# A two-layer pair kernel: x in halves from two queues, pair bias issued by ACT, third u ahead of the scores, channels innermost in the first centering, and idle TensorE products

## The reference

```python
x = x + attention(_gn(x), ...)         # 4 heads of 32
x = x + triangle(_gn(x), ...)

def attention(x):                      # layer norm, then
    xn = (x - mu) * rsqrt(var + 1e-05) * ln_gamma + ln_beta
    tri_bias = einsum('bijc,hc->bhij', xn, w_bias)
    q, k, v = projections of xn        # q scaled by 1/sqrt(32)
    scores = einsum('biqhd,bikhd->bihqk', q, k) + tri_bias[:, None] + mask_bias
    o = einsum('bihqk,bikhd->biqhd', softmax(scores), v) * sigmoid(xn wg + bg)
    return o wo + bo

def triangle(z):                       # layer norm, then
    a, b = mask * sigmoid(gate) * projection, twice
    x = einsum('bikh,bjkh->bijh', a, b)
    return sigmoid(zn g + g_b) * (layernorm(x) z_w + z_b)
```

## Time and profile before

| | us |
|---|---|
| median of 3 runs | 285.29 (284.13 to 285.58) |
| the profiled execution | 284.4 |
| its span | 282.6 |
| busy PE / DVE / ACT / POOL | 226.4 / 210.6 / 209.2 / 144.4 |

### The profile page before, as it was taken

The page is one execution under the profiler, slowest core; times in us unless marked ns, Lnnn a source line. Parts: engine busy times, 40 slices in busy tenths (PEclk is TensorE's granted clock), DMA queues, the critical chain, the costliest instruction groups (busy, mean ns, idle before and its releaser), DMA issues.

```text
span 282.6 us, 6859 instructions
## 1 busy us (share of the span) xinstructions
PE 226.4 (80%) x2394; PEld 182.6 (65%) x2394; DVE 210.6 (75%) x368; ACT 209.2 (74%) x953; POOL 144.4 (51%) x132
## 2 busy tenths in 40 slices
PE   0589492469999999999999999999669599677930
PEld 0579230347888878888788887888459566376930
DVE  4047962357999999999999999998545739959790
ACT  0566643279999999999999999999545645569590
POOL 5400000008876777767777677766200019998081
PEclk9999668579999999999999999999958689965695
DMA  8400033534454643554445553330000000000038
GB/s 130 63 11 2 1 112 121 171 124 142 145 171 170 221 163 132 199 181 165 165 149 195 184 186 118 117 115 2 0 2 0 0 2 2 1 1 2 0 49 118
DMA packets 42389, 27.09 MB, mean 96 GB/s; under 512 B 24404, under 2 KB 42356, under 8 KB 42356
## 3 DMA queue, kind: packets, MB, share of 16 engines
q1 hardware_dynamic: 36572, 25.95, 28.8%
q10 hardware_dynamic: 5784, 0.71, 1.7%
HBM read 1.36 MB, written 1.18 MB: 9 GB/s over the span
## 4 chain that ended last, share of the span: by engine, by line
PE 31%; issue 27%; ACT 21%; DVE 12%; POOL 4%; SPq 3%; POOLq 1%; DMA 0%; DVEq 0%; ACTq 0%
ACT maps L659 17%; PE psum L1181 7%; PE psum L1060 3%; PE psum L1192 3%; PE psum L1145 2%; SPq L392 2%; DVE u_full L951 2%; PE psum L1248 2%; PE psum L1171 2%; DVE shared L991 2%; PE psum L1226 2%; PE psum L1231 2%; PE psum L1146 1%; PE psum L1148 1%; PE psum L1257 1%
## 5 line engine op out<-in xcount | busy, mean ns | idle before, releaser
L659 ACT ACTIVATE maps<-psum,neg_max 96x96 f32<-96x96 f32 x384 | 123.9, 353 | 4.9 <-DVE neg_max L928 4.1
L490 POOL TENSOR_TENSOR maps<-maps,rden 96x768 f32<-96x768 f32 x48 | 70.5, 1469 | 81.5 <-DVE rden L938 75.3
L659 ACT ACTIVATION_READ_ACCUMULATOR maps<-psum,neg_max 96x1 f32 x384 | 83.9, 219 | 0.0
L944 DVE COPY turned<-psum 96x1024 f32<-96x1024 f32 x48 | 58.5, 1219 | 8.4 <-PE psum L1181 8.4
L928 DVE TENSOR_REDUCE neg_max<-psum 96x8 f32<-96x768 f32 x48 | 45.7, 953 | 5.1 <-PE psum L1148 4.9
L1145 PE MATMUL psum<-u_st,x_stack 128*96 128x384 f32 x96 | 37.8, 394 | 10.4 <-DVE bias_lo L913 8.1
L1181 PE MATMUL psum<-ident,maps 96*96 96x96 f32 x384 | 40.0, 247 | 0.3 <-POOL maps L490 0.3
L1146 PE MATMUL psum<-bias_hi,ident_r 128*96 128x384 f32 x96 | 33.7, 351 | 0.0
L1148 PE MATMUL psum<-bias_lo,ident_r 128*96 128x384 f32 x96 | 33.4, 348 | 0.0
L1181 PEld LDWEIGHTS psum<-ident,maps 96*96 96x96 f32 x384 | 32.0, 126 | 0.5 <-POOL maps L490 0.5
L1145 PEld LDWEIGHTS psum<-u_st,x_stack 128*96 128x96 f32 x96 | 15.9, 166 | 19.8 <-issue 10.5
(11 more groups left out here) (178 smaller groups left out, 424.1 us busy)
## 6 DMA issues: line engine op xcount, KB each, us to landing
u_st<-u_split SPq DMA_DIRECT2D x96, 192.0 KB
x_stack<-shared SPq DMA_DIRECT2D x40, 96.0 KB, 2.0
maps<-in_x SPq DMA_DIRECT2D x4, 288.0 KB, 5.1
x_stack<-shared SPq DMA_DIRECT2D x4, 144.0 KB, 2.1
out_y<-maps SPq DMA_DIRECT2D x6, 96.0 KB, 3.1
out_y<-maps ACTq DMA_DIRECT2D x6, 96.0 KB, 3.4
bias_lo<-gate_sb SPq DMA_DIRECT2D x24, 12.0 KB
x_stack<-shared SPq DMA_DIRECT2D x4, 48.0 KB, 1.9
```

The lines of the kernel that those rows point to most:

```text
L490: pool.tensor_tensor(at, at, rden[:, rows, :].unsqueeze(3).to_broadcast([N, 2, H, N]), ALU.mult).then_inc(probs_ready, 1)
L659: e = act.activation(probs[:, k % SLOTS, n, h], bank_s[r % 4][0:N, h * N:(h + 1) * N], ACT.Exp, bias=neg_max[:, r % BODY, h:h + 1], accum_ ...
L944: dve.tensor_copy(turned[0:N, j % 2].rearrange("p r x -> p (r x)"), psum[0:N, 2 * BANK:4 * BANK]).then_inc(t_ready, 1)
```

## The change

- x is loaded in two halves (12 of 24 blocks each): SP issues members 0 and 1, ACT members 2 and 3, ahead of its other loads. TensorE waits for each half by itself.
- The pair bias's four transfers are issued by ACT, behind its last bias copy, and no longer by SP behind `stage(0)`.
- The third u (`u_projection(2)`, its high and low part) comes ahead of the first scores, no longer behind the second.
- Layer 0's centred values lie as (f c) in the banks, as layer 1's do; the reduction reads them contiguously, the normalization writes them to the old place in (c f).
- TensorE gets products of `ones_r` and `tri_b`, 96 by 192, whose results nobody reads: 40 before x, 8 before the first means, 10 before the first centering, 20 before the first transposes, 36 before the first scores; in layer 1, 6 and 6 around the last output, 8 and 9 ahead of variance and centering, 28 behind the centering and 3 between quads of transposes. For them `ones_made` tells TensorE that `ones_r` is set.

```diff
@@ -164,10 +164,6 @@
-def by_layer(v, layer):
-    return v.rearrange("j b f c -> j b c f") if layer else by_blocks(v)
@@ -209,11 +205,12 @@
-x_loaded = [sem(f"x_loaded{f}") for f in range(GROUP)]
+x_loaded = [sem(f"x_loaded{half}") for half in range(2)]
...
+ones_made = sem("ones_made")
@@ -340,6 +337,9 @@
+IDLE = (40, 6, 8, 9, 28, 3, 6)
+IDLE_BANKS = (2, 6, 0)
+IDLE_FIRST = (8, 10, 20, 36)
@@ -383,14 +383,20 @@
+def load_x(eng, members_of_group):
+
+    for half in range(2):
+        at = slice(half * BLOCKS // 2, (half + 1) * BLOCKS // 2)
+        for f in members_of_group:
+            eng.dma_start(xt[:, at, f, :],
+                          x[0, f * BLOCKS:(f + 1) * BLOCKS][at].rearrange("b j c -> j b c")).then_inc(x_loaded[half], 16)
+
...
-    for f in range(GROUP):
-        sp.dma_start(xt[:, :, f, :],
-                     x[0, f * BLOCKS:(f + 1) * BLOCKS].rearrange("b j c -> j b c")).then_inc(x_loaded[f], 16)
+    load_x(sp, (0, 1))
     for n, v in enumerate(norm_rows):
@@ -432,9 +438,6 @@
     stage(0)
-    sp.wait_ge(bias_copied, QUADS)
-    for h in range(H):
-        sp.dma_start(pair_bias[:, h, :], bias_t[h * GROUP:(h + 1) * GROUP]).then_inc(bias_spread, 16)
     sp.wait_ge(parts_ready, QUADS)
@@ -534,6 +537,7 @@
 def _(act):
+    load_x(act, (2, 3))
     act.dma_start(mask_in[:, :], mask0[0]).then_inc(mask_loaded, 16)
@@ -643,6 +647,10 @@
+    act.wait_ge(bias_copied, QUADS)
+    for h in range(H):
+        act.dma_start(pair_bias[:, h, :], bias_t[h * GROUP:(h + 1) * GROUP]).then_inc(bias_spread, 16)
+
@@ -675,11 +683,11 @@
     high_part(1)
+    high_part(2)
...
                    ACT.Copy).then_inc(bias_copy, 1)
-    high_part(2)
     for k in range(STEPS):
@@ -750,7 +758,8 @@
     link(dve.memset(tri_b[:, :].bitcast(f32), 0.0))
-    link(dve.memset(ones_r[0:2, :].bitcast(f32), 1.0))
+    dve.memset(ones_r[0:2, :].bitcast(f32), 1.0).then_inc(ones_made, 1)
+    dve.wait_ge(ones_made, 1)
     dve.wait_ge(ident_made, 1)
@@ -788,13 +797,8 @@
         link(dve.reciprocal(by_channel(5), by_channel(4)))
-        scaled, unscaled = centering_r[:, :], centering[:, :, :]
-        if layer:
-            scaled = scaled.rearrange("p (f c) -> p f c", f=GROUP)
-            unscaled = unscaled.rearrange("p c f -> p f c")
-        else:
-            scaled = scaled.rearrange("p (c f) -> p c f", f=GROUP)
-        dve.tensor_scalar(scaled, unscaled, by_channel(5), None, ALU.mult).then_inc(centering_ready, 1)
+        dve.tensor_scalar(centering_r[:, :].rearrange("p (f c) -> p f c", f=GROUP),
+                          centering[:, :, :].rearrange("p c f -> p f c"), by_channel(5), None, ALU.mult).then_inc(centering_ready, 1)
         if not layer:
@@ -802,22 +806,14 @@
             dve.wait_ge(d_squared, QUADS * layer + q + 1)
-            ins = dve.tensor_reduce(tok[:, 0, at], by_layer(work, layer)[:, at].rearrange("j b c f -> j b f c"),
-                                    AX.X, ALU.add)
+            ins = dve.tensor_reduce(tok[:, 0, at], work[:, at], AX.X, ALU.add)
         link(ins)
...
             at = slice(4 * q, 4 * q + 4)
-            if layer:
-                dve.tensor_tensor(square[:, at],
-                                  banks[q][0:N, :].rearrange("j (b f c) -> j b f c", c=C, f=GROUP),
-                                  tok[:, 3, at].unsqueeze(3).to_broadcast([N, 4, GROUP, C]),
-                                  ALU.mult).then_inc(normed, 1)
-            else:
-                dve.tensor_tensor(by_blocks(square)[:, at],
-                                  banks[q][0:N, :].rearrange("j (b c f) -> j b c f", c=C, f=GROUP),
-                                  tok[:, 3, at].unsqueeze(2).to_broadcast([N, 4, C, GROUP]),
-                                  ALU.mult).then_inc(normed, 1)
+            to = square[:, at] if layer else by_blocks(square)[:, at].rearrange("j b c f -> j b f c")
+            dve.tensor_tensor(to, banks[q][0:N, :].rearrange("j (b f c) -> j b f c", c=C, f=GROUP),
+                              tok[:, 3, at].unsqueeze(3).to_broadcast([N, 4, GROUP, C]), ALU.mult).then_inc(normed, 1)
@@ -906,6 +902,7 @@
     low_part(1)
+    low_part(2)
@@ -964,7 +961,6 @@
-    low_part(2)
     minus_max(0)
@@ -1002,6 +998,14 @@
 def _(pe):
+    pe.wait_ge(ones_made, 1)
+
+    def idle_products(bank, count):
+
+        for _ in range(count):
+            pe.matmul(banks[bank][0:N, 0:PW + C], ones_r[:, :], tri_b[:, 0:PW + C], start=True, stop=True)
+
+    idle_products(IDLE_BANKS[0], IDLE[0])
     pe.wait_ge(ident_made, 1)
@@ -1035,8 +1039,14 @@
             for q in range(QUADS):
+                if 2 * q % QUADS == 0:
+                    pe.wait_ge(x_loaded[2 * q // QUADS], 16 * GROUP)
                 raw_transposes(q)
         mean = averaging[:, :, :].rearrange("p f c -> p (f c)")
+        if layer:
+            idle_products(IDLE_BANKS[0], IDLE[1])
+        else:
+            idle_products(7, IDLE_FIRST[0])
         if layer:
@@ -1046,11 +1056,15 @@
                 res_transposes(q)
+            idle_products(IDLE_BANKS[0], IDLE[2])
         pe.wait_ge(chan_squared, layer + 1)
...
             second_weights()
+            idle_products(IDLE_BANKS[0], IDLE_FIRST[1])
+        else:
+            idle_products(IDLE_BANKS[0], IDLE[3])
@@ -1068,6 +1082,7 @@
             pe.matmul(bank_w[0:N, HD:2 * HD], beta_wide, z_weights, start=False, stop=True).then_inc(z_prep_mm, 1)
+            idle_products(IDLE_BANKS[1], IDLE[4])
@@ -1080,6 +1095,8 @@
         mm.then_inc(transposed, 1)
+        if layer and q < QUADS - 1:
+            idle_products(IDLE_BANKS[2], IDLE[5])
@@ -1102,13 +1119,12 @@
     pe.wait_ge(consts_made, CONSTS)
-    for f in range(GROUP):
-        pe.wait_ge(x_loaded[f], 16)
     norm_front(0)
...
     to_groups(slice(PW, PW + 2), norm_in[:, :], ident[0:6, 2:4]).then_inc(tri_stack_mm, 1)
+    idle_products(6, IDLE_FIRST[2])
     pe.wait_ge(tri_stack_copied, 1)
@@ -1195,6 +1211,8 @@
         if k % 2 == 0 and 0 <= y < BLOCKS:
+            if y == BLOCKS - 1:
+                idle_products(IDLE_BANKS[0], IDLE[6])
             pe.wait_ge(o_ready, y + 1)
@@ -1207,12 +1225,13 @@
     u_projection(1)
+    u_projection(2)
+    idle_products(6, IDLE_FIRST[3])
     pe.wait_ge(zeroed, ZEROED)
...
     scores_of(1)
-    u_projection(2)
     pe.wait_ge(bias_copy, 1)
```

## The result

The changed kernel takes 281.17 us (median of four runs; one of them, at 303.56, ran at a lower clock throughout and is left out of the ratio, and the median of the other three is 281.02) against 284.96: ratio 0.986, 95% interval 0.982 to 0.990. It is faster, by some 3.9 us and not by the 7.7 that were forecast. The profiled execution took 281.3 us (284.4 before), with a span of 279.4 (282.6).

A forecast was written before the change was run, and what follows sets the result against it. Open to gain were the sequential phases before and behind the ACT-paced attention loop, with TensorE's clock often low. 284.4 - 3.4 (front) - 4.3 (second layer) = 276.7, with 0.9 for the median 277.6 us; range 274.0 to 283.2.

The forecast's parts named there:

- first rival: Clock lost among first transposes as before: front gives nothing, second layer its 4.3 us, 281.0 us in all; chance 0.27.
- part 3: First layer's transposes and bias products: 20 idle products keep the clock full, 8.2 us instead of 11.6, -3.4 us.
- Part 1: Loading x from two queues: ACT's issues delay its loads, table load and copies, +1.3 us, bounds +0.3 and +2.5.
- Part 2: First centering: ten idle products cost time, higher clock and contiguous reduction save more, -0.3 us, bounds -0.6 and +1.7.
- Part 4: Pair bias and third u before the scores: first exponential at 53.8 instead of 58.18 us, -4.4; idle products end the wait.
- Part 5: Second layer's front: idle products hold the clock through centering, transposes and first projection, -4.3 us.
- The loop: Attention loop between the two fronts: ACT works without pause at full clock, length unchanged at 140 us.

The follow-up runs named there:

- no_36: The changed kernel without the 36 idle products ahead of the first score, all other idle products kept: 279.90 us, ratio 0.979 to before.

## Why the prediction held its range and missed its size

It was the first rival, with 0.27, that came: the clock lost among the first transposes, the front giving nothing (first exponential at 58.2 by its reckoning, 58.58 measured), the second layer its 4.3; 281.0 against 281.17. That the two times agree to 0.2 us is in part luck: the rival started from 285.3, where the median is now 284.96, and the profile has 1.0 us more in the loop. The sign and the range held, the range because it took that rival in. The forecast of 277.6 failed in one step.

**The step that failed: part 3.** "20 idle products, so the clock is kept: -3.4" gave 0. From the first transpose to the end of the last bias copy it is 11.53 us; before, 11.61. The argument was that the gap ahead of the transposes had lost the clock, and that filling it would keep it. The 20 products ran at full clock, and it fell 3 us behind them, among transposes; TensorE had been at work for 8.3 of the 10.2 us at full clock. The gap was shortened from 3.88 to 1.37 us and not filled, and two more of 0.30 and 0.41 us came with the strided write. Of five traces with the 20 products and none between the transposes the clock was kept in one (no_36, with the same gaps); with 36 products ahead and five behind each quad, and no gap at all, it was kept in all three.

What lost it stays open between two causes. One is what the prediction quoted against itself: by the Trainium skill (TensorE: Matmul & The Clock Gate, Part 4: PE-mode transpose) transposes don't count as busy in the same way. For it speaks that TensorE was at work for 6.7 of the 6.9 us from 34.6 on at half clock (6.71 us busy in the window 34.6 to 41.5), as it was in before from 31.99. Against it, the clock rose at 41.5 (at 40.6 in before) while TensorE had had nothing but these transposes and bias products for 8.5 us, and no_36 kept it through all of them. The other is the remaining gaps: every trace that lost the clock has them, and the three gapless ones kept it. A run with 36 products ahead and contiguous writes, but none between the transposes, would come nearer to parting them. I gave the loss 4 in 10; the half clock on a busy TensorE in the rows of before should have had the larger share.

**Its size was bounded too high as well.** no_36 shows what a kept clock gives: 8.5 us instead of 11.5, nearly the 8.2 reckoned, and then the second u waits 5.4 us for the stacking of x; its first exponential is at 58.36. The term needed the transfers behind it.

**Part 1**, +1.3 forecast: +1.02. ACT's issue 3.98 us (4.2), first copy 12.98 (12.5), last loads 11.55 (11.0). The six copies then went at 0.46 us instead of 0.64, since all their transposes were long done. What the step lacked was the comparison with halves from SP alone, -2.2. The Trainium skill (Perfetto Trace Analysis, DMA Optimizations) says that splitting DMAs may let some work start sooner; the run agrees, with TensorE at 6.32 us. It also says that balancing issues over engines may help where descriptor generation is the bottleneck; here it brought x in 2 us sooner (all of it by 7.75, against 9.84 for the second half from SP alone) and cost 3.0 us, since ACT's own loads and table stood behind it. No run shows that making descriptors was the bottleneck. The part's premise that two queues close holes only was low: from 4 to 7 us they moved 215 to 216 GB/s, against 201 to 203 at most from one in before.

**Part 2**, -0.3: DVE's token sums are complete 0.77 us later than before with 1.02 from part 1, so -0.25. The reduction took 0.68 us. The strided write costs 0.31 us a quad, inside its bounds of 0 to 0.45, but not where I put it: "ahead of TensorE's pace" was wrong, TensorE waits three times, the first transpose comes 1.03 us later than before, so that nothing of the 0.25 is left there, and the split behind it starts at 37.29 instead of 34.65, the stacking with it.

**Part 4** in its own length: last bias copy to first exponential 14.0 us, 13.6 forecast, 14.6 before. Issue 3.4 (3.1), two rounds of u 1.9 each (1.66), 36 products 4.95 (5.2), score to exponential 2.2 (2.1). "Idle products, not the bias, end the wait" held. What I didn't ask is whether they pay: without the first layer's products the score comes 3.8 us earlier, and the full clock returns 1.4.

**Part 5**, -4.3: -4.34 in the profile, of which -2.4 up to the last square (-2.1 forecast) and -1.95 behind it (-2.2). Without its 72 products the stretch is 5.0 us longer and the time about 4.

**The loop** was to be unchanged. It is 1.04 us longer in this profile (139.7), and 138.3 to 139.4 us in the other twelve traces of edited kernels, whose loops are the same; the second trace of the changed kernel has 138.5. So I take it for the scatter of single executions, and what makes it stays open. It also means that the first exponentials, and not the spans, are what two traces of fronts can be compared by. Open too is why the clock rises at 24.4 us in one execution and at 27.5 in another with the same instructions ahead of it, and so why it was kept in no_36.

## What to carry to other kernels

Products that only hold TensorE's clock pay where they fill waits that are there anyway and the work behind them is TensorE's own (4.3 us here for 72 products); ahead of a short piece of work, in a place where another engine could already be served, they cost more than they return, so each group is tested by itself. Among transposes with gaps the clock was lost four times in five with the same 20 products ahead, so don't count on it there. Before a queue is shared with an engine that computes, look what that engine does next: four DMA issues on ACT moved its table load and every copy behind them, while splitting the same load in two on SP alone was worth 2.2 us.

## What the runs showed of the hardware

- Idle products on operands that are zero but for two rows lift the clock, and in the second layer they hold it: it rose to full at 7.3 us, during the first 40 (at 23.5 before), and in the second layer it stayed full from 206.6 to 227.0. One costs 0.085 us at full clock and 0.17 at half (10 in 1.9 us, 28 in 2.77, with the last one's latency), as estimated.
- An early full clock doesn't last: it fell at 14.1, behind the raw transposes, and was at half when the first centering came.
- DVE's 96x512 product from PSUM written with a stride of four elements takes 1.08 us (0.91 us from one start to the next), contiguous 0.68 (0.60 from start to start).
- Four issues of 144 KB each take 3.98 us on ACT while SP issues as many in 3.31; eight on SP alone take 6.42, and four of twice the size 6.36. So the bytes count and not the number of issues; whether the transfers or the making of their descriptors sets it, no run tells. What else is under way counts too, in staging u: 2.5 us alone and in most traces behind ACT's bias transfers (3.5 in that of the changed kernel), 5.4 beside POOL's.
